# Later rows of x loaded behind named matmuls, and one batch's small products moved between its value matmuls, in a cross-attention and ternary FFN kernel

## The reference

```
x = x + xattn(layernorm(x), ctx, ctx, mask)
x = x + ffn(layernorm(x))

xattn: q, k, v = heads(query @ Wq.T + bq), heads(key @ Wk.T + bk), heads(value @ Wv.T + bv)
       q' = relu(q @ Wqf.T); k' = relu(k @ Wkf.T) * mask          # 32 -> 64 features
       kv = sum over rows of k' (x) v ; k_sum = sum over rows of k'
       out = (q' @ kv) / (q' @ k_sum + 1e-8);  return out @ Wo.T + bo
ffn:   gate, up = bit_linear(x, w_gate), bit_linear(x, w_up)      # rows to 8 bits, weights to -1, 0, 1
       a = up * square(relu(gate)); a = a * rsqrt(mean(a^2) + 1e-6) * subln_weight
       return bit_linear(a, w_down)
```

## Time and profile before

| | before |
|---|---|
| median of 3 runs | 427.86 us (427.54 to 429.09) |
| time of the profiled execution | 430.05 us |
| its span | 428.0 us |
| PE busy | 414.2 us (97%), 4835 matmuls |
| DVE busy | 341.2 us (80%) |
| ACT busy | 287.0 us (67%) |
| POOL busy | 145.4 us (34%) |
| granted TensorE clock | 1.00 throughout |

### The profile page before, as it was taken

The page is one execution under the profiler, slowest core; times in us unless marked ns, Lnnn a source line. Parts: engine busy times, 40 slices in busy tenths (PEclk is TensorE's granted clock), DMA queues, the critical chain, the costliest instruction groups (busy, mean ns, idle before and its releaser), DMA issues.

```text
span 428.0 us, 11266 instructions
## 1 busy us (share of the span) xinstructions
PE 414.2 (97%) x4835; PEld 282.6 (66%) x4835; DVE 341.2 (80%) x505; ACT 287.0 (67%) x406; POOL 145.4 (34%) x290
## 2 busy tenths in 40 slices
PE   7989999997999999999999999999999999999995
PEld 5889889986878855844764575575467566464443
DVE  4544849566939949998987897999998898998983
ACT  5674989892145277779539647764883978939970
POOL 0000000002433732384281545536225533444660
DMA  7992656543202010023313033031303121423055
GB/s 219 416 415 87 233 214 214 233 156 144 101 5 87 38 26 2 12 51 87 71 40 64 0 87 74 14 74 40 64 31 61 34 49 21 84 71 65 11 121 150
DMA packets 51170, 42.42 MB, mean 99 GB/s; under 512 B 43056, under 2 KB 44080, under 8 KB 49200
## 3 DMA queue, kind: packets, MB, share of 16 engines
q1 hardware_dynamic: 51120, 41.70, 32.3%
HBM read 27.01 MB, written 4.19 MB: 73 GB/s over the span
## 4 chain that ended last, share of the span: by engine, by line
PE 58%; DVE 17%; ACT 8%; POOL 6%; issue 5%; DMA 5%; SPq 0%; DVEq 0%; POOLq 0%; ACTq 0%
PE ps L353 48%; DVE zb L359 3%; DVE rows_of L365 3%; PE ps L561 2%; PE ps L683 2%; POOL tk L362 2%; PE ps L588 2%; ACT rb L356 2%; DMA xs<-in_wu_dram 2%; PE ps L660 2%; DVE tk L767 2%; ACT kT L356 2%; POOL zb L359 1%; DMA xqT<-xqb 1%; PE ps L622 1%
## 5 line engine op out<-in xcount | busy, mean ns | idle before, releaser
L353 PE MATMUL ps<-tg,xqT 128*128 128x512 bf16 x256 | 60.6, 380 | 0.8 <-DMA xqT<-xqb 0.7
L353 PE MATMUL ps<-tu,xqT 128*128 128x512 bf16 x256 | 60.6, 379 | 0.2 <-DVE zb L359 0.2
L362 POOL TENSOR_SCALAR tk<-tk 128x1 f32<-128x1 f32 x96 | 39.4, 411 | 36.9 <-DVE tk L718 19.4
L353 PE MATMUL ps<-td,yqT 128*128 128x512 bf16 x208 | 46.9, 379 | 0.0
L353 PEld LDWEIGHTS ps<-tu,xqT 128*128 128x128 bf16 x256 | 24.3, 98 | 31.1 <-issue 2.1
L356 ACT ACTIVATE rb<-zb 128x1024 f32<-128x1024 f32 x29 | 30.6, 1055 | 21.0 <-DVE zb L359 20.9
L353 PEld LDWEIGHTS ps<-tg,xqT 128*128 128x128 bf16 x256 | 23.5, 98 | 30.8 <-issue 2.5
L359 DVE TENSOR_TENSOR zb<-ps,rb 128x1024 f32<-128x1024 f32 x29 | 35.3, 1217 | 6.8 <-ACT rb L356 6.7
L353 PE MATMUL ps<-aph,wkh 128*128 128x256 f32 x128 | 36.2, 287 | 1.5 <-DVE wkl L359 0.6
L353 PE MATMUL ps<-aph,wqh 128*128 128x256 f32 x128 | 37.1, 290 | 0.0
L767 DVE TENSOR_REDUCE tk<-zb 128x1 f32<-128x1024 f32 x30 | 36.2, 1207 | 1.1 <-POOL zb L359 0.8
(11 more groups left out here) (134 smaller groups left out, 1052.2 us busy)
## 6 DMA issues: line engine op xcount, KB each, us to landing
xs<-in_wg_dram SPq DMA_DIRECT2D x4, 1024.0 KB, 13.1
xs<-in_wu_dram SPq DMA_DIRECT2D x4, 1024.0 KB, 6.2
xs<-in_wd_dram SPq DMA_DIRECT2D x4, 1024.0 KB, 7.8
xs<-in_x_dram SPq DMA_DIRECT2D x8, 512.0 KB, 4.5
out_dram<-xs SPq DMA_DIRECT2D x15, 256.0 KB, 2.1
craw<-in_ctx_dram SPq DMA_DIRECT2D x7, 512.0 KB, 7.5
xs<-in_wk_dram SPq DMA_DIRECT2D x4, 256.0 KB, 4.7
xs<-in_wv_dram SPq DMA_DIRECT2D x4, 256.0 KB, 6.8
```

The source lines that it names most:

```text
L353: return add("pe", name, cost, waits, lambda e: e.matmul(out, lhsT, rhs, start=start, stop=stop))
L362: return add(lane, name, cost, waits, lambda e: e.tensor_scalar(out, a, s1, s2, op0, op1))
```

## The change

Three edits. The loads of x2 to x5 wait, besides for their slot, for `v7.1.0.0`. The loads of x6 and x7 wait, besides for their slot, for `end1`. And for batch 1 the products of batch 0 are run after the first half of the values, not before it.

```
-                        dma(f"x{n}", 0.5, slot_user[n // 2], xs[:, 2 * n:2 * n + 2, :], x_d[n], f"x{n}")
+                        dma(f"x{n}", 0.5, slot_user[n // 2] + ([f"v{NB - 1}.1.0.0"] if n >= 2 else []), xs[:, 2 * n:2 * n + 2, :], x_d[n], f"x{n}")
...
-            if b:
-                run_all(kv(b - 1))
+            older = kv(b - 1) if b else []
+            late = b == 1
+            if not late:
+                run_all(older)
             means(b, "kv")
             run_all(values(b, 0))
+            if late:
+                run_all(older)
             run_all(values(b, 1))
...
-                        dma(f"x{b}", 0.5, slot_user[b // 2], xs[:, 2 * b:2 * b + 2, :], x_d[b], f"x{b}")
+                        dma(f"x{b}", 0.5, slot_user[b // 2] + [end1], xs[:, 2 * b:2 * b + 2, :], x_d[b], f"x{b}")
```

## The result

| | before | changed |
|---|---|---|
| median, 22 runs each | 428.70 us (427.44 to 429.65) | 427.08 us (426.44 to 429.09) |
| ratio of the times | | 0.9978 (95% interval 0.9970 to 0.9987) |
| the same ratio, timed twice more (12 runs each) | | 0.9949 (0.9926 to 0.9972), 0.9974 (0.9954 to 0.9995) |
| profiled execution | 430.05 us, span 428.0 | 426.96 us, span 424.9 |

The change makes the kernel faster by 0.22%, or 0.9 us, under the 0.5% that I named as the border; I had forecast 426.0 us, 0.43% under the three runs shown. The medians alone stand 1.62 us apart: the 22 times of the kernel before fall in two groups, ten from 427.44 to 428.06 us and twelve from 428.69 to 429.65, and their median lies at the low end of the upper one. Two later executions of the kernel before, of 463 and 586 us, are left out of all that follows. The two profiled executions stand 3.1 us apart in span.

A forecast was written before the change was run, and what follows sets the result against it. PE was taken to bound the kernel (busy 414.2 of 428.0 us), with 4.57 us of issue stalls from late program blocks. Terms 1.75 + 0.2 - 0.1 = 1.85 us off the 427.86 median gave 426.0, range 424.4 to 427.7.

The forecast's parts named there:

- The count of 128 matmuls: Between PE's issue stalls: 128 matmuls, 256 instructions with weight loads, so the program arrives in blocks and stalls where one is late.
- the border after 66 in `features(1)`: With kv(0) moved, the next block is late at matmul 66 of features(1): a new stall of 0.8 us.
- `kv(5)` and P7 in one piece: Signs of success: the stalls of 1.84 us at about 101 and 0.85 us at 141.62 are gone.
- the wait for `xqT0`: Before G0.0: PE arrives 0.85 us earlier, then idles until the DMA of xqT ends.
- the term of `kv(5)`: x2 to x5 later: of the 1.84 us stall at 101.48, 1.75 taken back; bounds 1.84 and 0.
- the moved `kv(0)`: Batch 0's products behind batch 1's first values: 0.69 us stall gone, new 0.8 stall; net -0.1, bounds +0.69 and -1.3.
- That chain doesn't hang on the stall: Chain to xqT0 before G0.0 follows POOL adds ahead of P7, so x6 and x7 later gain 0.2 of 0.85 us.
- I cost it at 0: Statistics of x2 to x5 in DVE's idle time before 126.44: cover just enough, a rest up to 0.6 us costs nothing.
- the sum: 1.75 + 0.2 - 0.1 = 1.85 us off the profiled execution, span 428.0 to 426.15.
- The first, everything pays: Stalls in kv(5), kv(0) and P7 all gained: 1.84 + 0.69 + 0.85 = 3.4 us, time 424.5; chance 0.22.
- The second: Stalls at 101.48 and 141.62 not made by loads, or return, or gain eaten: 0 to 1.2 us, 427.4; chance 0.18.
- The third: Slower by one DVE wait on x6's load before xq0.b, up to 3.7 us late, 429.7; chance 0.08.

The follow-up runs named there:

- the warming test: The kernel before with 9 warming matmuls at the start in place of 13; breaks moved from 90 to 94, 98 to 102, 107 to 111; no time given.
- the break made at will in P6: Change without moved kv(0), x2 to x5 waiting for the second half of batch 6's values; 0.9960 of before (0.9942 to 0.9977), P6 break 0.55 us.

## Why the prediction came out as it did

**Right: what the stalls are, and where each goes.** The count of 128 matmuls, the border after 66 in `features(1)`, `kv(5)` and P7 in one piece and the wait for `xqT0` came as worked out. One reading was loose: DMA at 98 to 104 us is full to about 100 and not 101, so the data of x0, x1 and Wo ends sooner than the 98.3 that I worked out, which only makes the term of `kv(5)` safer. The Trainium skill (Runtime: NRT & Kernel Launch, Instruction fetch mechanics) gives blocks of 16 KiB, 256 instructions, which the moved borders bear out to the matmul; that their refill is mostly hidden holds in the quiet parts only.

**Right in size, within chance: two terms.** Taken from the parts' timings with the clock held: x2 to x5 1.8 us where I had 1.75; the moved `kv(0)` 0.56 lost alone, and nothing beside the later loads on one chip, where I had 0.1, inside my bounds.

**Wrong: "That chain doesn't hang on the stall".** x6 and x7 gave 0.5 us where I had 0.2. I read the chain to `xqT0` from one execution. The four other profiles of the kernel before (one of them with 9 warming matmuls) show 18.2 to 18.6 us from the start of F7 to G0.0 (135.74 to 153.99 in the one of 432.1 us) where that one has 17.3 (134.43 to 151.76), and with x6 and x7 late it is 16.9 to 17.2 in nine of eleven profiles. The layer norm of the next tile (`xn`, L362) waits for X3 behind P7, and DVE's fixed order has it ahead of `xq0`. Timeline of DVE before, in the execution of 430.05 us and in that of 428.43 us:

```profile
143.56 0.55 DVE L362 TENSOR_SCALAR xn<-xs,mv,rstd 128x512 f32<-128x512 f32 x1 [0.50 <-PE ps L622]
```

```profile
141.22 1.50 DVE L362 TENSOR_SCALAR xn<-xs,mv,rstd 128x512 f32<-128x512 f32 x1 [0.72 <-PE ps L622]
```

With a break of 0.80 or 0.85 us in P7 this step takes 0.55 us, and G0.0 comes 17.3 us after F7 starts (two profiles); with 0.90 to 1.07 it starts within 0.1 us of an add of POOL, takes 1.48 to 1.66 us, and G0.0 comes about 1 us later (four profiles). In the chain that ended last of the execution of 428.43 us this step stands between the break in P7 and `xqT0`. So the break does reach G0.0, and where it is long it costs more than itself.

**Wrong: "I cost it at 0".** The statistics in their new place, and the `bo` load behind them, I took to cost nothing; three of ten profiles have the stop in F7, of 1.0 us where it could be measured beside its twin.

**Wrong: the step from the sum to the time.** I wrote "428.0 to 426.15 of span", noted that this execution stood 2.2 us over the median, and then took the whole 1.85 off that median: "427.86 - 1.85 = 426.0". This is the step that failed. A term that is a break must be sized for the executions against which it is set. The one profiled had breaks of 4.57 us in sum; one of 428.43 us has 3.1 in sum, with 0.73 us and not 1.84 in `kv(5)`. The break in `kv(5)` measured 0.73 to 2.03 us over seven profiles. The 427.86 of the three runs is a time of the lower of the two groups, to which 10 of the first 22 times belong and only 5 of the 62 later ones with the clock held (under 428.1 us). The changed kernel's 426.96 us is the profiled 430.05 less 3.1; set against the three runs of 427.86, it is 0.9 less, and the ratio over 22 runs, 0.9978, lies there. In the later timings the kernel before stands at 429.0 with the clock held, while the changed one stays at 426.9 to 427.3; against that base the sum would have given 427.1. That agreement is in part luck, since one term was too small and a cost was missing. Why the kernel before was quicker in the first timings stays open, as no execution of it under 428.4 us was profiled. The two groups lie some 1.2 us apart, and 0.73 and 1.84 us in `kv(5)` 1.1, which fits a short break there, but executions of 428.29 and 428.81 us of kernels with the loads of x2 to x5 early have long ones.

**Not in the prediction at all: the clock.** None of my rivals had the clock fall behind a long break. It fell in 24 of 86 later executions of before (where it was looked at, behind the break in `kv(5)`, 1.6 us once), and it is why the loads without `kv(0)` gave 2.7 and 3.0 us in the median and 2.2 with the clock held.

**The rivals.** The first, everything pays, was wrong at `kv(0)`, right in part for P7, whose break does reach G0.0. The second, to which the Trainium skill's rule would have led, falls by the warming test and by the break made at will in P6. The third didn't come: in the changed kernel's profile DVE doesn't wait for x6 before `xq0.b`.

## What to carry to other kernels

Where PE idles by "issue", count its instructions between two such stops. If they are 256 or a multiple, look at what DMA carries in the 3 to 6 us before: move large loads away from stages of very small matmuls, and when a dense stage itself is moved, follow the next border too, since it is asked for later and may be needed sooner. Size a stall from several executions before it is taken off a median.

## What the runs showed of the hardware

- PE's program came in blocks of 256 instructions. With DMA idle, the transfer of the next one was seen 1.05 and 1.1 us after the border before was passed, and in the changed kernel it was there when PE needed it, about 3.8 us after that border (`kv(5)` takes 1.53 us there and 1.40 in three other profiles of the later loads). Behind a load PE went on 4.6 us (96.15 to 100.70) to 6.2 us after that border. A stage of 128 products takes 1.4 us, one of 128 features 1.6.
- Behind an idle stretch of 2.03 us (and one of 1.76) the granted clock fell to 1.2 GHz for about 3.5 us; behind stretches of 1.84, 1.82 and 1.76 us in other executions it did not.
- 1 MB less in the start of the kernel ended the full stretch of DMA at 29.2 and not at 31.6 us, and the breaks at 21 and 27 us still stood, with 0.85 and 0.69 us.
